# Expert stage of a fused embedding kernel: gated chunks in a ring of eight quads, and the finished code read from PSUM and biased by VectorE

## The reference, cut to what matters

```python
z = jnp.einsum('nd,sdr->nsr', xf, P)                 # 8 subspaces of 16
scores = jnp.einsum('nsr,smr->nsm', z, C)            # 64 experts in each
topv, topi = jax.lax.top_k(scores, K)                # the best 4
w = jax.nn.softmax(topv, axis=-1)
...
h = jax.nn.gelu(jnp.einsum('nsr,nskrh->nskh', z, W1g) + b1g)   # 32 hidden units
yl = jnp.einsum('nskh,nskhr->nskr', h, W2g) + b2g
comb = jnp.einsum('nskr,nsk->nsr', yl, w)            # the code, 128 values
out = jax.nn.gelu(comb @ G1 + g1b) @ G2 + g2b
```

## Time and profile before

| | us |
|---|---|
| median of 3 runs (lowest, highest) | 1747.78 (1738.67, 1751.03) |
| the profiled execution | 1759.2 |
| span in its profile | 1757.5 |
| stage 3, from its first hidden product to the end of the span | 920 |
| one tile of stage 3, mean of ten | 75.2 |

### The profile page before, as it was taken

The page is one execution under the profiler, slowest core; times in us unless marked ns, Lnnn a source line. Parts: engine busy times, 40 slices in busy tenths (PEclk is TensorE's granted clock), DMA queues, the critical chain, the costliest instruction groups (busy, mean ns, idle before and its releaser), DMA issues.

```text
span 1757.5 us, 28838 instructions
## 1 busy us (share of the span) xinstructions
PE 1499.6 (85%) x8184; PEld 660.6 (38%) x8184; DVE 1178.0 (67%) x3230; ACT 1038.0 (59%) x2151; POOL 1045.9 (60%) x770
## 2 busy tenths in 40 slices
PE   5971889988998898885898898998989899898996
PEld 3630556665556666653122222222222222222222
DVE  4462367777787777777576666666667666676664
ACT  0131333433444444342787878888888787887875
POOL 4550245565565555554576767667676676767764
PEclk9755789998999999996799999999999999999998
DMA  7337101111211111214121221213212131221300
GB/s 230 94 93 91 30 27 49 51 57 49 72 48 58 48 48 51 69 47 109 46 56 36 58 50 38 66 31 71 55 38 55 35 78 40 53 49 38 79 21 14
DMA packets 93333, 102.15 MB, mean 58 GB/s; under 512 B 12215, under 2 KB 90575, under 8 KB 93007
## 3 DMA queue, kind: packets, MB, share of 16 engines
q1 hardware_dynamic: 89945, 96.01, 22.6%
q0 software_dynamic: 2112, 3.79, 0.8%
q10 hardware_dynamic: 1232, 1.84, 0.3%
HBM read 64.83 MB, written 33.52 MB: 56 GB/s over the span
## 4 chain that ended last, share of the span: by engine, by line
PE 64%; DVE 18%; issue 8%; ACT 3%; POOL 3%; DMA 2%; SPq 1%; DVEq 0%; POOLq 0%; ACTq 0%
PE code L1586 20%; PE ring L1572 19%; PE ring L1458 4%; DVE arena L1137 3%; DVE arena L1336 3%; DVE arena L1339 3%; PE ring L1430 2%; PE ring L1429 2%; PE ring L1469 2%; PE code L1489 2%; PE ring L1489 2%; DVE arena L1126 2%; DVE arena L1117 1%; PE ring L1379 1%; DVE arena L1212 1%
## 5 line engine op out<-in xcount | busy, mean ns | idle before, releaser
L779 POOL TENSOR_TENSOR arena<-arena 128x992 f32<-128x992 f32 x264 | 602.9, 2295 | 283.9 <-ACT arena L972 127.2
L1572 PE MATMUL ring<-arena,w_stack 99*128 99x496 bf16 x1536 | 429.3, 387 | 89.6 <-DVE arena L1339 46.9
L972 ACT ACTIVATE ring<-ring 128x992 f32<-128x992 f32 x444 | 429.4, 984 | 97.5 <-PE ring L1572 96.6
L1336 DVE TENSOR_TENSOR arena<-ring,arena 128x496 f32<-128x496 f32 x576 | 358.2, 667 | 127.8 <-ACT ring L972 71.0
L1586 PE MATMUL code<-arena,w_pad 128*32 128x496 f32 x3072 | 408.1, 605 | 0.0
L1339 DVE TENSOR_TENSOR arena<-ring,arena 128x992 f32<-128x992 f32 x216 | 255.2, 1186 | 142.6 <-PE code L1586 99.7
L1572 PEld LDWEIGHTS ring<-arena,w_stack 99*128 99x128 bf16 x1536 | 125.6, 98 | 535.1 <-DVE arena L1336 212.6
L972 ACT ACTIVATE arena<-ring 128x992 f32<-128x992 f32 x204 | 203.6, 998 | 16.3 <-PE ring L1572 12.1
L1586 PEld LDWEIGHTS code<-arena,w_pad 128*32 128x32 f32 x3072 | 61.6, 109 | 141.1 <-issue 133.0
L1458 PE MATMUL ring<-arena 128*32 128x93 f32 x768 | 74.8, 316 | 40.2 <-DVE arena L1212 40.2
L711 POOL TENSOR_TENSOR arena<-arena 128x372 f32<-128x372 f32 x96 | 91.8, 975 | 27.5 <-DVE arena L1181 27.1
(11 more groups left out here) (134 smaller groups left out, 1980.4 us busy)
## 6 DMA issues: line engine op xcount, KB each, us to landing
arena<-gates SPq DMA_DIRECT2D x48, 496.0 KB, 6.7
gates<-arena SPq DMA_DIRECT2D x16, 744.0 KB, 10.1
arena<-h_scratch SPq DMA_DIRECT2D x32, 279.0 KB
arena<-z_parts SPq DMA_DIRECT2D x144, 62.0 KB, 2.2
h_scratch<-arena SPq DMA_DIRECT2D x16, 279.0 KB
z_parts<-arena SPq DMA_DIRECT2D x48, 93.0 KB, 1.7
arena<-h_scratch SPq DMA_DIRECT2D x12, 372.0 KB
out_h<-arena SPq DMA_DIRECT2D x12, 372.0 KB
```

The lines of the kernel that those rows point to most:

```text
L779: p_.tensor_tensor(gated[:, block % 2, j, 2 * a:2 * a + 2], hid[:, POOL_DUOS.index(duo) % 2], gst[:, block // EB, j].unsqueeze(1).to_broad ...
L972: a_.activation(product if to_pool is None else to_pool, product, ACT.Gelu_apprx_tanh).then_inc(s_hid, 1)
L1336: v_.tensor_tensor(gated[:, block % 2, j, 2 * a + k], duo_bank(duo, k), gst[:, block // EB, j], ALU.mult).then_inc(s_gat, 1)
L1572: mm = t_.matmul(duo_bank(duo, k), w1s[:, x:x + 128], zst[:, o, j], start=True, stop=True)
```

## The change

- **Order of the chunks.** A quad is now one k of all four pairs j; its first duo is the pairs 0 and 1, its second the pairs 2 and 3 (`parts`). So a decode reads exactly one quad. `gated` is a ring of eight quads (`SPACES`) in the same amount of SBUF. A gate of quad q waits for the decode of quad q - 8 (`first_of_quad`), and a decode for its own quad's second duo.
- **TensorE's order.** At quad q it issues duos 2q and 2q + 1 and then the decode of quad q - 4 (`LAG`). `out1` comes after duo 21, `out2` after duos 27 and 31, which are the same places of the ring as before, so the 10 duos at its end are the same.
- **Who gates.** GpSimd again has 22 duos, others than before: 4, 7, 9, 12, then 15, 18, 20, 23, and so on in steps of 11. VectorE has 42, now each in two instructions of one bank (84 of the L1336 kind for 48 of it and 18 of the L1339 kind).
- **The code.** `copy_code` and its buffer are gone, and GpSimd's `add_bias`. VectorE adds the bias from the `code` bank in one instruction after its gate before duo 8; the decode that opens the next tile in that bank waits for it (`s_cb`).
- **VectorE's `add_out`** stands after duos 27 and 31 (before: 25 and 29).

```diff
-POOL_DUOS = [d for d in range(DUOS) if d % 3 == 0]
-DVE_LIST = [d for d in range(DUOS) if d not in POOL_DUOS]
+POOL_DUOS = [d for d in range(4, DUOS) if d % 11 in (1, 4, 7, 9)]
+DVE_DUOS = [d for d in range(DUOS) if d not in POOL_DUOS]
 RING = 7
-AHEAD = 4
-BIAS_AFTER = 12
-OUT1_AT, OUT2_AT = 8, (11, 13)
+LAG = 4
+SPACES = 8
+BIAS_AFTER = 7
+OUT1_AT, OUT2_AT = 21, (27, 31)
...
-            if d == 2 * q + AHEAD + 1:
+        for at, name in ((OUT1_AT, "f1"), (OUT2_AT[0], "f2_0"), (OUT2_AT[1], "f2_1")):
+            if d == at:
...
-SPLIT = [d for d in DVE_LIST if d % 2 == 0 or d in WRAPS]
-DVE_GATES = len(DVE_LIST) + len(SPLIT)
...
-    before = sum(1 + (d in SPLIT) for d in DVE_LIST if d < duo)
-    own = 0 if duo not in DVE_LIST else 1 + piece if duo in SPLIT else 1
-    return DVE_GATES * tile + before + own
+    before = sum(d < duo for d in DVE_DUOS)
+    return 2 * (len(DVE_DUOS) * tile + before) + (1 + piece if duo in DVE_DUOS else 0)
...
+def first_of_quad(duo, mine):
+    return duo % 2 == 0 or duo - 1 not in mine
+def parts(duo):
+    quad = duo // 2
+    block, k = divmod(quad, KH)
+    return quad, block, k, 2 * (duo % 2)
...
-        gated = c3(128, [2, PAIRS, KH, TN])
-        comb = c3(128, [TN])
+        gated = c3(128, [SPACES, PAIRS, TN])
...
-                quad, a = divmod(duo, 2)
-                block, j = divmod(quad, PAIRS)
+                quad, block, k, j = parts(duo)
                 if duo == first_pool[block // EB]:
                     pool.wait_ge(s_gl[block // EB], 32 * (tile + 1))
-                if first_of_half_block(duo, POOL_DUOS):
-                    wait(pool, s_code, QUADS * tile + PAIRS * (block - 2) + 2 * a + 2)
+                if first_of_quad(duo, POOL_DUOS):
+                    wait(pool, s_code, QUADS * tile + quad - SPACES + 1)
                 pool.wait_ge(s_hid, DUOS * tile + duo + 1)
-                p_.tensor_tensor(gated[:, block % 2, j, 2 * a:2 * a + 2], hid[:, POOL_DUOS.index(duo) % 2],
-                                 gst[:, block // EB, j].unsqueeze(1).to_broadcast([128, 2, TN]),
-                                 ALU.mult).then_inc(s_pg, 1)
-            def add_bias(tile):
-                wait_apart(pool, (s_comb, tile + 1), (s_bl, 16 * (tile + 1)))
-                p_.tensor_tensor(code, comb, bias_t, ALU.add).then_inc(s_cb, 1)
+                p_.tensor_tensor(gated[:, quad % SPACES, j:j + 2], hid[:, POOL_DUOS.index(duo) % 2],
+                                 gst[:, block // EB, j:j + 2], ALU.mult).then_inc(s_pg, 1)
...
-            def copy_code(tile):
-                act.wait_ge(s_code, QUADS * (tile + 1))
-                a_.copy(comb, code_bank[:, 0:TN]).then_inc(s_comb, 1)
...
-                        if duo == 9:
-                            copy_code(tile - 1)
-                        if duo == 2 * OUT1_AT + 5:
+                        if duo == OUT1_AT:
...
             def gate_duo(tile, duo):
-                quad, a = divmod(duo, 2)
-                block, j = divmod(quad, PAIRS)
+                quad, block, k, j = parts(duo)
                 if duo == first_dve[block // EB]:
                     dve.wait_ge(s_gl[block // EB], 32 * (tile + 1))
-                if first_of_half_block(duo, DVE_LIST):
-                    wait(dve, s_code, QUADS * tile + PAIRS * (block - 2) + 2 * a + 2)
+                if first_of_quad(duo, DVE_DUOS):
+                    wait(dve, s_code, QUADS * tile + quad - SPACES + 1)
                 dve.wait_ge(s_hid, DUOS * tile + duo + 1)
-                if duo in SPLIT:
-                    for k in range(2):
-                        v_.tensor_tensor(gated[:, block % 2, j, 2 * a + k], duo_bank(duo, k),
-                                         gst[:, block // EB, j], ALU.mult).then_inc(s_gat, 1)
-                else:
-                    v_.tensor_tensor(gated[:, block % 2, j, 2 * a:2 * a + 2], duo_banks(duo),
-                                     gst[:, block // EB, j].unsqueeze(1).to_broadcast([128, 2, TN]),
-                                     ALU.mult).then_inc(s_gat, 1)
+                for p in range(2):
+                    v_.tensor_tensor(gated[:, quad % SPACES, j + p], duo_bank(duo, p),
+                                     gst[:, block // EB, j + p], ALU.mult).then_inc(s_gat, 1)
+            def add_bias(tile):
+                dve.wait_ge(s_code, QUADS * (tile + 1))
+                dve.wait_ge(s_bl, 16 * (tile + 1))
+                v_.tensor_tensor(code, code_bank[:, 0:TN], bias_t, ALU.add).then_inc(s_cb, 1)
...
+                        if duo == BIAS_AFTER:
+                            add_bias(tile - 1)
                         for half in range(2):
-                            if duo == 2 * OUT2_AT[half] + 3:
+                            if duo == OUT2_AT[half]:
...
-                quad, a = divmod(duo, 2)
-                block, j = divmod(quad, PAIRS)
-                o, hb = divmod(block, EB)
+                quad, block, k, j = parts(duo)
+                o, eb = divmod(block, EB)
                 if duo % (DUOS // 2) == 0:
                     pe.wait_ge(s_zl[o], 96 * (tile + 1))
-                for k in range(2):
-                    bank_free(tile, (duo, k))
-                    x = chunk(2 * j + o, hb, 2 * a + k) * 128
-                    mm = t_.matmul(duo_bank(duo, k), w1s[:, x:x + 128], zst[:, o, j],
+                for p in range(2):
+                    bank_free(tile, (duo, p))
+                    x = chunk(2 * (j + p) + o, eb, k) * 128
+                    mm = t_.matmul(duo_bank(duo, p), w1s[:, x:x + 128], zst[:, o, j + p],
                                    start=True, stop=True)
                 mm.then_inc(s_hp1, 1)
-            def decode(tile, block, k):
-                if k % 2 == 0:
-                    needed = 2 * (PAIRS * block + PAIRS - 1) + k // 2
-                    pe.wait_ge(s_gat, dve_gated(tile, needed))
-                    pe.wait_ge(s_pg, pool_gated(tile, needed))
-                if k == 0 and block == 0:
-                    wait(pe, s_comb, tile)
+            def decode(tile, quad):
+                pe.wait_ge(s_gat, dve_gated(tile, 2 * quad + 1))
+                pe.wait_ge(s_pg, pool_gated(tile, 2 * quad + 1))
+                if quad == 0:
+                    wait(pe, s_cb, tile)
+                block, k = divmod(quad, KH)
                 o, eb = divmod(block, EB)
                 for j in range(PAIRS):
                     mm = t_.matmul(code_bank[32 * j:32 * j + 32, 0:TN], w2p[:, chunk(2 * j + o, eb, k)],
-                                   gated[:, block % 2, j, k], start=(block == 0 and k == 0),
-                                   stop=(block == BLOCKS - 1 and k == KH - 1), skip_group_check=True)
+                                   gated[:, quad % SPACES, j], start=(quad == 0), stop=(quad == QUADS - 1),
+                                   skip_group_check=True)
                 mm.then_inc(s_code, 1)
...
-            def tile_pe(tile, first, last):
-                def hidden_ahead(quad, ahead):
-                    duo = 2 * quad + ahead
-                    if duo < DUOS:
+            def tile_pe(tile, first):
+                for quad in range(QUADS):
+                    for duo in (2 * quad, 2 * quad + 1):
                         hidden(tile, duo)
-                    elif not last:
-                        hidden(tile + 1, duo - DUOS)
-                def decode_next(quad):
-                    block, k = divmod(quad - PAIRS, KH)
-                    if block >= 0:
-                        decode(tile, block, k)
+                        if not first:
+                            if duo == OUT1_AT:
+                                out1(tile - 1, tile)
+                            for half in range(2):
+                                if duo == OUT2_AT[half]:
+                                    out2(tile - 1, half, tile)
+                    if quad >= LAG:
+                        decode(tile, quad - LAG)
                     elif not first:
-                        decode(tile - 1, BLOCKS - 1, k)
-                for quad in range(QUADS):
-                    hidden_ahead(quad, AHEAD)
-                    hidden_ahead(quad, AHEAD + 1)
-                    decode_next(quad)
-                    if not first:
-                        if quad == OUT1_AT:
-                            out1(tile - 1, tile)
-                        for half in range(2):
-                            if quad == OUT2_AT[half]:
-                                out2(tile - 1, half, tile)
-            for duo in range(AHEAD):
-                hidden(0, duo)
-            tile_pe(0, True, False)
-            with pe.Fori(1, TILES - 1) as tile:
-                tile_pe(tile, False, False)
-            tile_pe(TILES - 1, False, True)
-            for k in range(KH):
-                decode(TILES - 1, BLOCKS - 1, k)
+                        decode(tile - 1, quad - LAG + QUADS)
+            tile_pe(0, True)
+            with pe.Fori(1, TILES) as tile:
```

(18 more changed lines are left out.)

2 lines of the change are left out of this document (1 added, 1 removed).

## The result

| | before | after |
|---|---|---|
| median, us | 1743.2 | 1650.1 (1645.9 to 1654.7, 4 runs) |
| ratio | | 0.947, 95% interval 0.941 to 0.952 |
| span in the profile, us | 1757.5 | 1646.8 |
| first hidden product of stage 3, us | 837.4 | 826.1 |
| stage 3, from there to the end of the span, us | 920.1 | 820.7 |

The forecast was 1649 with a gain of 99 us. Stage 3 became 99.4 us shorter. The medians differ by 93, the spans by 111: stages 1 and 2, whose code is the same, end anywhere from 814 to 837 us in the traces of this study. The latest is the kernel before, with a mean granted clock of 0.85 over these stages; the changed kernel has 0.87. So times of the whole execution scatter by some 1%, and what follows is read mostly from stage 3 and its tiles.

A forecast was written before the change was run, and what follows sets the result against it. No engine was full; TensorE, nearest, needed 64.0 of 75.17 us a tile. Terms summed to -8.5, so 66.7 a tile: 93 us over eleven tiles, 4.5 in the first, 1.1 at the end, together 99, giving 1649 us (1630 to 1690).

The forecast's parts named there:

- Block edges, 5.2 a tile: VectorE's gates wait for a decode to free half of `gated`, TensorE then for VectorE's banks; 5.2 us a tile removed.
- The 1.71 at the output: TensorE's loss around `out2`, put down to a block edge and `add_out` placed too early; all 1.71 us a tile dropped.
- TensorE's own 64.0: TensorE's need per tile: 32 quads at 1.91 us, 61.1, plus 2.9 for `out1` and both halves of `out2`.
- The wait for the code, 1.80: ScalarE's copy of the code after gelu 9 waits 1.45 us for the decode; TensorE's loss of 1.80 us a tile goes.
- New stall before decode 0, 0.9: Next tile's decode 0 waits for VectorE's add of the bias: 0.9 us more a tile, bounds 0 and 2.0.
- Clock, 1.26: TensorE's fall to the lower clock level, once a tile, disappears from steady tiles: 1.26 us a tile gained.
- The rival in which it falls once a tile: TensorE's clock still falls in every tile, costing 14 us: 1663 us; chance 0.16.
- the longest gaps at 0.9: Reason given for the clock staying up: TensorE's longest remaining gaps would be 0.9 us, with no run of gaps.
- The run of five VectorE duos, 0.3: At the tile's end and start, duos 63, 0, 1, 2, 3 without GpSimd: 1.4 us at most, 0.3 taken.
- VectorE's pieces: Split gates: two instructions take 1.25 us together, 0.3 a tile lost; rival 1.33, giving 1676 us, chance 0.08.
- Sum: All terms together: -8.5 us a tile, so 66.7; 99 us off the whole kernel.

The follow-up runs named there:

- the two-step path in the changed kernel: Changed kernel with ScalarE copying the code to SBUF after gelu 7 and GpSimd adding the bias after its duo 9: 1638.2 us, ratio 0.943.
- the version with 1.7 us of wait before decode 0: Changed kernel with GpSimd's duos of before (every third from 0), VectorE's add of the bias now behind gate 7: 1648.8 us, ratio 0.945.

## Why the prediction was right, step by step

- **Block edges, 5.2 a tile:** right: no distance of that kind is left in the changed kernel's tiles. That they held TensorE is shown by the ring of four quads, which put waits of that kind back and cost 7.2 a tile where 7 were worked out. The way of working it out (product to gelu 0.51, gelu to gate 1.02, gate to bank 0.74) carried.
- **The 1.71 at the output:** the size was right, the cause only in part. The prediction gave it to a block edge and to the place of the adds. In the kernel before the first add did not wait, and the 2.78 us of the second cost TensorE nothing; moved early in the changed kernel, the adds cost 0.3. The step that failed is the reading of a wait of VectorE as a loss of TensorE: the rows gave the time of VectorE's wait, not who was held.
- **TensorE's own 64.0:** somewhat high. The prediction took the 0.98 of `out1` for each half of `out2` as well. A half costs 0.65 where nothing holds it (2.56 less 1.91, with GpSimd's list of before) and 0.95 in the changed kernel.
- **The wait for the code, 1.80:** right. The code path alone, in the old kernel, took it out. But its cause is the place of the copy in ScalarE's queue, not the engine, as the two-step path in the changed kernel shows.
- **New stall before decode 0, 0.9:** 0.87 of idle time, 1.01 from decode to decode. Right in size and place. With the add a gate later it was 1.76 (1.8 worked out), with the add before gate 7 it was gone.
- **Clock, 1.26:** right in that it stays up in the changed kernel, and somewhat low in size: a tile with a fall is 1.6 to 1.7 us longer than one without, in both versions that have the two kinds. The rival in which it falls once a tile did not come. How near it was shows the version with 1.7 us of wait before decode 0, where it fell in four tiles of ten. The reason on record, "the longest gaps at 0.9", did not hold: the loop end had gaps of up to 1.5 us, and the clock stayed up. The rule of the Trainium skill on short idle spells between groups that cycle through PSUM banks (TensorE: Matmul & The Clock Gate, "A second HAM failure mode: psum-queue depth-cycling") fits the kernel before, with its one fall a tile, and not the ring of four quads, whose TensorE idled in most quads at a clock of 1.00.
- **The run of five VectorE duos, 0.3:** the size was near on the mean, the mechanism was not. In tiles without the jump it costs nothing (the wrap takes 0.82 in all). In tiles with it VectorE stands 2.26 us for its next instructions, and TensorE loses 1.6 and then 0.4. With 0.3 less before decode 0 such a tile is 1.7 longer, 0.7 on the mean over the tiles. The rows of before had no hint of it: the jump fell where duos 63 and 0 were GpSimd's.
- **VectorE's pieces:** two take 1.25 as in the earlier trace rows, four 2.42, so a further piece adds 0.58. The fixed cost that the Trainium skill gives for each instruction (VectorE: DVE Perf Modes, "The TRN2 errata") agrees with the time of one piece alone: 668 ns measured, 674 by an estimate from its figure. In full for each piece, as an estimate, it would make two take 1.35, and that did not come. Nor did splitting bring anything, except at the wrap.
- **Sum:** 66.7 a tile against 66.9, 0.8 against 0.72 us from the last add to `out1`, 99 against 99.4 for the stage. So close a hit is in part luck. A tile without the jump takes 66.2, half a microsecond less than forecast, and the jump, which nobody had foreseen, puts it back. The ten tiles between the `out1` products gave 82.4 us where 85 were forecast, the rest of the stage 17.0 where 14. And the profiled span was to be 1658.5 and was 1646.8; that the median fell within 1 us of 1649 all the same lies inside what stages 1 and 2 scatter.

## What to carry to other kernels

List the starts of one repeated instruction of the fullest engine, subtract its undisturbed distance, and give each excess to a wait; then check by experiment that the wait was the holder, since an engine's idle time is a loss only if the fullest engine stands behind it. A buffer that is read by block and written by block couples the engines at each edge; a ring in the order in which it is read removes this with the same memory. Before moving work to another engine, look whether the work waits because of its place in the queue: one duo earlier may be worth more than one engine fewer.

## What the runs showed of the hardware

- VectorE stood 2.26 us at the jump of its loop, 1.4 of them after its input was ready; it did so in every second tile, and writing the loop out removed it. Giving the engine no due work at the jump hid it fully, 65.2 to 65.3 us in every tile, as long as TensorE paused at the wrap; without that pause 0.5 to 0.7 us a jump came back.
- With the loop written out the stall went, but VectorE's gates started 0.11 us behind the gelu they waited for, where it had been 0.04, and the mean stayed at 66.9 us.
- The granted clock of TensorE stayed at 1.00 through a stage with a wait of 0.15 us or more in most of its quads, and through gaps of 1.4 and 1.5 us at VectorE's loop end. It fell in four of ten tiles with a gap of 1.69 us before decode 0, and not in the other six. A fall made a tile 1.6 to 1.7 us longer. Which gap brings one down is not settled here.
